# A decoder's first self attention rewritten from pairs of heads to quads of heads, with the rotation's partner shuffled instead of projected

## The chip, the core and the metric

One Trainium2 chip, one of its cores. The metric is device time in microseconds from the first to the last instruction of the launch, as the median of several runs. TensorE runs at one of two granted clocks, 1.2 or 2.4 GHz; the profile gives the mean over a stretch as a share of 2.4 GHz.

## The reference

The kernel computes six blocks of a decoder of depth two on x of shape (8, 256, 256) in float32: each normalises x and adds its result to it. The change touches the first block alone, self attention of 64 query heads of 16 values (4 branches of 16 heads) over 16 key heads that the branches share:

```python
q, k = _rope(q), _rope(k)
scores = einsum('bhtd,bhsd->bhts', q, k) * ATTNSCALE
key_self = clip(sum(k * k, axis=-1), 1e-06, None)
w = softplus(scores / sqrt(key_self)[:, :, None, :])
w = where(causal, w, 0.0)
w = w * sigmoid(SCALE * w)
w = where(w < sinks, 0.0, w)
total = sum(w, axis=-1) + sinks + 1e-06
out = einsum('bhts,bhsd->bhtd', w / total, v) + sinks / total * v_null
y = mean over branches of (out @ W_O + W_O_bias)
```

## The kernel before

`attention0` (lines 247 to 690) first normalises all of x and turns it (`normalise`, which also issues the stage's loads and waits for them in `loaded`), then works through 8 batches with all engines side by side. Every engine has its own in-order list of work; semaphores tie the lists together. A batch's 16 key heads are taken in 8 steps of a **pair of heads**, and two steps make a **quad**.

For each pair there are three score slots (`score_slot`), each two PSUM banks of 512 columns in banks 0 to 5. A slot is two matmuls of 32 rows (L335 or L342: the two heads lie in two row groups of 32 rows, which TensorE can use at the same time) and two matmuls of all 128 rows that add the causal mask (L338, 256 columns, or L345, 512 columns). Each float32 matmul is two instructions in the trace. ScalarE takes each slot with a softplus into the weights `w` (`soften`, L464), and after six slots it loads another table and runs four silu instructions over the quad (L502), then loads the softplus table again. VectorE cuts the weights at the sinks, sixteen instructions for a quad (`threshold`, L674). TensorE then sums over the keys (`sum_half`, L365, four column groups of 32 at once), two halves for a quad.

Beside this main line there are **side items**, which pass through banks 6 and 7: the projections q and k of a batch, projected twice, once as they are and once with the halves of each head swapped (weights `wq` and `wqs`, `wk` and `wks`, L393), which VectorE turns into two products with cosine and sine (L623) and GpSimd adds (L551); v (L400, L631); the norms of the keys (L406, L636, then Ln and Exp on ScalarE, L510 and L512, and L582 on GpSimd); the sums copied by ScalarE (L483), transposed back by TensorE ("regroup", L413) and copied by VectorE (L644, with the totals at L654 and L658); the contexts divided by GpSimd (L570, L577), transposed ("turn", L420, taken by ScalarE at L473) and projected out (L427, L663). Which item goes to TensorE at which step stands in the tables `SENT` and `SENT_LATE`; where VectorE takes it, in `TAKEN`. A bank of side items may be written again when its reader is done (`free`). The batches overlap: a step can hold an item of the batch before (`OLD`) or after (`AHEAD`). The weights `w` have room for four pairs (`PAIR_RING`).

Of the kernel before, what the change touches and what calls it, by code (L numbers as in the profile page):

```python
# [11 lines left out]
ALU = mybir.AluOpType  # L12
# [121 lines left out]
def normalise(nc, norm, x_all, xnT_all, ident, psum, loads, loaded):  # L134

    with ExitStack() as stack:
# [64 lines left out]
PAIRS_OF_HEADS, QUADS, SLOTS = NH // 2, NH // 4, 3  # L201
PAIR_RING = 4
# [16 lines left out]
SENT_LATE = {0: ("regroup", 4, OLD, 6), 1: ("regroup", 5, OLD, 7), 2: ("regroup", 7, OLD, 6), 3: ("norm", 0, AHEAD, 7),  # L219
             4: ("q", 0, AHEAD, 7), 5: ("q", 1, AHEAD, 6), 6: ("q", 3, AHEAD, 7), 7: ("regroup", 2, HERE, 6)}  # L220

SUM_BANKS = {1: (7, 6), 3: (7, 6), 5: (6, 7), 7: (6, 7)}

EVEN_POINTS, ODD_POINTS = 6, 3
TAKEN = {(0, 0): ("regroup", 2, OLD, 6), (0, 1): ("regroup", 3, OLD, 7), (0, 2): ("q", 0, HERE, 6), (0, 3): ("q", 1, HERE, 7),
         (0, 4): ("q", 2, HERE, 6), (0, 5): ("q", 3, HERE, 7), (1, 0): ("regroup", 4, OLD, 6),
         (2, 0): ("regroup", 5, OLD, 7), (2, 1): ("k", 0, AHEAD, 6), (2, 2): ("k", 1, AHEAD, 7), (2, 3): ("v", 0, HERE, 6),
         (2, 4): ("regroup", 6, OLD, 7), (3, 0): ("regroup", 7, OLD, 6),
         (4, 0): ("norm", 0, AHEAD, 7), (4, 4): ("regroup", 0, HERE, 6), (5, 0): ("q", 0, AHEAD, 7),
         (6, 0): ("q", 1, AHEAD, 6), (6, 3): ("out", 0, OLD, 6), (6, 4): ("regroup", 1, HERE, 7), (6, 5): ("q", 2, AHEAD, 6),  # L230
         (7, 0): ("q", 3, AHEAD, 7)}
REGROUPS = 8
ROTATED = 2 + 2 * BR


def rotations(b, kind, i, when):

    place = i if when == HERE else 4 + i if kind == "k" else 6 + i
    return b * ROTATED + 6 + place


def quad_at(b, at, new, old):

    if at >= 0:
        return (at, b * QUADS + at) if new else None
# [2194 lines left out]
```

## Time and profile before

| what | us |
|---|---|
| median of 3 runs | 3093.82 (3092.99 to 3099.23) |
| the profiled execution: its time | 3088.96 |
| its span, first to last instruction | 3087.2 |
| the first attention: last load landed to its last instruction | 29.45 to 925.48 |

The profile's shares of busy time over the whole span are TensorE 88%, VectorE 57%, ScalarE 51%, GpSimd 26%; they average over six blocks with different limits. To read it for this change, take the stretch from 25 to 960 us alone, see which engine is busy in it and what the others wait for, and then follow one quad in the timeline.

### The profile page before, as it was taken

The page shows a single profiled execution, that of the slowest core. Times are in us where ns is not written, and L with a number is a line of the kernel's source. Part 1 is how long each engine was busy: PE and PEld are TensorE (multiplying, and loading weights), DVE is VectorE, ACT ScalarE, POOL GpSimd, SP SyncE. Part 2 cuts the span into 40 slices and gives each one's busy share as a digit, 9 for nine tenths or more (in the row PEclk, how much of TensorE's full clock was granted, in tenths as well). Part 3 has the DMA queues.
Part 4 walks back from the last instruction along what each step waited for, and adds up shares of the span by engine and source line. Part 5 has one row for each costly group of instructions (what it writes and reads, how often), then busy time and mean ns, then how long its engine had stood idle before and what let it go on. Part 6 is the DMA issues. An engine that isn't in the chain of part 4 may idle for free. (4 is left out here: it accounts for less than half of the span.)

```text
span 3087.2 us, 46929 instructions
## 1 busy us (share of the span) xinstructions
PE 2711.5 (88%) x17384; PEld 2026.2 (66%) x17384; DVE 1762.0 (57%) x4040; ACT 1559.8 (51%) x3054; POOL 788.5 (26%) x887
## 2 busy tenths in 40 slices
PE   6889888988867689999979999999979999949998
PEld 3444444544436467776758888888867777748887
DVE  3555545544547566556546666666666565555454
ACT  2665656565645344444435555555555556542221
POOL 1122222212210144444531111111005566610000
PEclk8888988987979799999989999999989999979999
DMA  3000000000002211111010000000010000020000
GB/s 104 4 4 4 1 4 4 4 1 4 1 1 66 77 25 25 30 44 25 22 34 13 6 6 6 3 1 1 1 67 8 6 7 5 1 96 6 6 8 31
DMA packets 88753, 58.80 MB, mean 19 GB/s; under 512 B 55120, under 2 KB 78544, under 8 KB 88016
## 3 DMA queue, kind: packets, MB, share of 16 engines
q1 hardware_dynamic: 88528, 55.80, 6.1%
q8 instruction: 142, 2.33, 0.3%
q14 instruction: 83, 0.68, 0.1%
HBM read 39.00 MB, written 8.39 MB: 15 GB/s over the span
## 5 line engine op out<-in xcount | busy, mean ns | idle before, releaser
L674 DVE SCALAR_TENSOR_TENSOR a_w<-a_w,a_sinks 128x384 f32<-128x384 f32 x512 | 324.2, 698 | 69.8 <-ACT a_w L502 69.8
L464 ACT ACTIVATE a_w<-psum 128x1024 f32<-128x1024 f32 x192 | 190.7, 1026 | 299.4 <-PE psum L338 119.1
L1103 POOL TENSOR_SCALAR f_weights<-f_weights,f_sums 128x256 f32<-128x256 f32 x256 | 232.8, 927 | 271.3 <-DVE f_sums L1333 271.3
L2011 POOL TENSOR_SCALAR x_weights<-x_weights,x_sums 128x256 f32<-128x256 f32 x256 | 232.5, 927 | 271.4 <-DVE x_sums L2070 271.4
L1261 ACT ACTIVATE f_weights<-psum,f_negmax 128x256 f32<-128x256 f32 x256 | 118.0, 473 | 210.3 <-DVE f_negmax L1327 210.3
L1597 ACT ACTIVATE a_turned_w_hi<-psum 128x512 fp32r<-128x512 f32 x256 | 139.1, 595 | 151.7 <-PE psum L1507 151.7
L1981 ACT ACTIVATE x_weights<-x_masked_s,x_negmax 128x256 f32<-128x256 f32 x256 | 127.0, 497 | 136.2 <-DVE x_negmax L2062 136.2
L1713 DVE TENSOR_REDUCE a_negmax<-psum 128x1 f32<-128x1024 f32 x128 | 156.7, 1224 | 64.6 <-PE psum L119 60.5
L502 ACT ACTIVATE a_w<-a_w 128x1536 f32<-128x1536 f32 x128 | 179.4, 1472 | 0.4
L335 PE MATMUL psum<-a_qT,a_kT_half 32*128 32x512 f32 x512 | 160.3, 705 | 15.9 <-ACT a_w L464 13.9
L1675 POOL TENSOR_TENSOR a_xT_lo<-all_xnT_all,a_xT_hi 128x512 fp32r<-128x512 f32 x56 | 71.5, 1277 | 384.8 <-ACT a_xT_hi L1577 384.8
L1720 DVE TENSOR_TENSOR a_turned_w_lo<-psum,a_turned_w_hi 128x512 fp32r<-128x512 f32 x256 | 163.7, 681 | 0.2 <-ACT a_turned_w_hi L1597 0.2
L117 PE MATMUL psum<-a_turned_w_hi,a_v_hi 128*128 128x256 f32 x512 | 150.1, 293 | 0.5 <-DVE a_turned_w_lo L1720 0.5
L118 PE MATMUL psum<-a_turned_w_lo,a_v_hi 128*128 128x256 f32 x512 | 144.8, 283 | 0.0
L119 PE MATMUL psum<-a_turned_w_hi,a_v_lo 128*128 128x256 f32 x512 | 144.8, 283 | 0.0
L1606 ACT ACTIVATE a_weights<-psum,a_negmax 128x1024 f32<-128x1024 f32 x128 | 143.5, 1121 | 2.3 <-DVE a_negmax L1713 2.2
L365 PE MATMUL psum<-a_w,a_v 128*32 128x512 f32 (+1 forms) x1024 | 120.3, 599 | 17.1 <-DVE a_w L674 14.2
L1507 PE MATMUL psum<-all_ident,a_weights 128*128 128x128 f32 x1024 | 132.6, 272 | 0.5 <-ACT a_weights L1606 0.5
L623 DVE SCALAR_TENSOR_TENSOR a_rot<-psum,a_bq,a_rope 128x256 f32<-128x256 f32 x128 | 55.6, 475 | 133.1 <-PE psum L393 133.1
L1507 PEld LDWEIGHTS psum<-all_ident,a_weights 128*128 128x128 f32 x1024 | 119.1, 140 | 17.8 <-ACT a_weights L1606 2.2
L570 POOL TENSOR_TENSOR a_ctxn<-a_ctx,a_vnull 128x256 f32<-128x256 f32 x64 | 45.8, 737 | 296.4 <-DVE a_ctx L644 296.4
L117 PE MATMUL psum<-a_kT_hi,a_qT_hi 128*128 128x512 f32 x256 | 106.5, 416 | 7.9 <-issue 6.9
(359 smaller groups left out, 7464.1 us busy)
## 6 DMA issues: line engine op xcount, KB each, us to landing
f_xnT<-all_xnT_all SPq DMA_DIRECT2D x16, 256.0 KB, 2.4
f_pv_rows<-f_pv SPq DMA_DIRECT2D x8, 512.0 KB, 3.2
f_pv_groups<-f_pv_rows SPq DMA_DIRECT2D x8, 512.0 KB
f_w<-in_f_w SPq DMA_DIRECT2D x2, 2048.0 KB, 9.9
all_x_all<-in_x SPq DMA_DIRECT2D x1, 2048.0 KB, 8.6
a_xnT<-all_xnT_all SPq DMA_DIRECT2D x8, 256.0 KB, 2.3
x_xnT<-all_xnT_all SPq DMA_DIRECT2D x8, 256.0 KB, 2.3
x_ctxT<-in_x_ctxT SPq DMA_DIRECT2D x8, 256.0 KB, 2.9
```

The source lines that it names most:

```text
L117: pe.matmul(out, lhsT[0], rhs[0], start=start, stop=False)
L118: pe.matmul(out, lhsT[0], rhs[1], start=False, stop=False)
L119: return pe.matmul(out, lhsT[1], rhs[0], start=False, stop=stop)
L335: pe.matmul(psum[:, 2 * x + h, :], kT_half[rows[h], step % 2, g, 0:P], qT[rows[h], g, 2 * x:2 * x + 2, :], start=True, stop=False)
L464: act.activation(to, of, ACT.Softplus).then_inc(softened, 1)
L502: act.activation(wu, wu, ACT.Silu, scale=SILU_SCALE).then_inc(silu_done, 1)
L674: ins = dve.scalar_tensor_tensor(part, part, sinks[:, col:col + 1], part, ALU.is_ge, ALU.mult)
L1103: ins = pool.tensor_scalar(w, w, sums[:, k, h, t:t + 1], None, ALU.mult)
L1507: ins = pe.transpose(psum[:, 4 + half, j * P:(j + 1) * P], weights[u % 2][:, lo:lo + P], ident[:])
L1713: dve.tensor_reduce(negmax[:, u % STAT_RING:u % STAT_RING + 1], psum[:, 2 * (u % 2):2 * (u % 2) + 2, :].rearrange("p a n -> p (a n)"), AX. ...
L1720: dve.tensor_tensor(lo, psum[:, 4 + half, :].rearrange("p (j t) -> p j t", t=P), hi.bitcast(F32), ALU.subtract)\
L2011: ins = pool.tensor_scalar(w, w, sums[:, k, h, t:t + 1], None, ALU.mult)
```

## The change

The first attention is issued anew; what it computes stays. One iteration m is now a whole quad of heads (`ALL_QUADS` = 32).

- **Score groups.** Three groups of four banks each (`scores`): four matmuls of 32 rows in the four row groups, into four banks, then four mask matmuls. `heads_of` pairs heads so that a quad's heads lie in the four row groups. Groups 0 and 2 of quad m use four banks (`banks_of(m)`), group 1 and the next quad's group 0 the other four. All eight banks serve scores; the number of instructions for scores stays.
- **Side items** now use fixed banks inside the four that the quad's last group has left (`beside_quad`, "first" before the sums and "last" after them), and every group of scores claims all four of its banks: it waits until softplus or the side items' readers have left them (`claim`).
- **The ring** of weights is 3 quads (4 pairs before). The sums of quad m - 1 are made in iteration m.
- **Rotation.** The swapped projections, their weights and their loads are gone. VectorE swaps the halves of each head out of PSUM with one shuffle instruction of 128x512 for two chunks (`stream_shuffle`), then makes the products; the bank is free after the first two of four products (`proj_taken`). GpSimd adds two chunks in one instruction.
- ScalarE takes the sums after silu, and names the silu table load; v is projected from `xnT_all` itself, and SyncE's copy into `xnT` is gone; the output projection is two items of one tile.

The diff, cut to its core:

```diff
-PAIRS_OF_HEADS, QUADS, SLOTS = NH // 2, NH // 4, 3
-PAIR_RING = 4
+QUADS, SLOTS = NH // 4, 6
+QUAD_RING = 3
...
-SENT = {0: [("regroup", 3, OLD, 7), ("q", 0, HERE, 6), ("q", 1, HERE, 7), ("q", 2, HERE, 6), ("q", 3, HERE, 7)],
-        2: [("k", 0, AHEAD, 6), ("k", 1, AHEAD, 7), ("v", 0, HERE, 6), ("regroup", 6, OLD, 7)],
-        4: [("turn", 0, OLD, 6), ("turn", 1, OLD, 7), ("turn", 2, OLD, 6), ("turn", 3, OLD, 7), ("regroup", 0, HERE, 6)],
-        6: [("out", 0, OLD, 6), ("regroup", 1, HERE, 7), ("q", 2, AHEAD, 6)]}
...
-SUM_BANKS = {1: (7, 6), 3: (7, 6), 5: (6, 7), 7: (6, 7)}
...
+ALL_QUADS = B * QUADS
...
+SWAP = [u // DH * DH + (u + DH // 2) % DH for u in range(32)]
...
+def heads_of(k):
+
+    return slice(8 * (k // 2) + k % 2, 8 * (k // 2) + 8, 2)
...
+def banks_of(m):
+
+    return m % 2 * 4
...
+def beside_quad(m):
+
...
+    if k == 0:
+        sent = [[("regroup", m - 2, 0, 0), ("regroup", m - 2, 1, 1), ("q", b, 2, 2)], [("out", b - 2, 1, 1)]]
+    elif k == 1:
+        sent = [[("v", b, 0, 0), ("q", b, 3, 1), ("regroup", m - 2, 0, 2)], [("regroup", m - 2, 1, 1), ("k", b + 1, 0, 2)]]
+    elif k == 2:
+        sent = [[("turn", b - 1, 0, 0), ("turn", b - 1, 1, 1), ("norm", b + 1, 0, 2)],
+                [("turn", b - 1, 2, 1), ("turn", b - 1, 3, 2), ("regroup", m - 2, 0, 3), ("regroup", m - 2, 1, 0),
+                 ("q", b + 1, 0, 1)]]
+    else:
+        sent = [[("regroup", m - 2, 0, 0), ("regroup", m - 2, 1, 1), ("q", b + 1, 1, 2)], [("out", b - 1, 0, 1)]]
+    made = lambda kind, of: 0 <= of < (ALL_QUADS if kind == "regroup" else B)
+    return [[(kind, of, i, banks_of(m) + bank) for kind, of, i, bank in part if made(kind, of)] for part in sent]
+
+
+SUM_BANKS = 3, 0
+SPAN = range(1 - QUADS, ALL_QUADS + QUADS + 1)
+
+TURNED_AT = {item[:3]: n for n, item in enumerate(
+    item for m in SPAN for part in beside_quad(m) for item in part if item[0] in "qk")}
 
 
 def attention0(nc, norm, x_all, xnT_all, ident, psum, a):
     with ExitStack() as stack:
         s = Scope(nc, stack, "a0")
-        wq, wqs = s.sb("wq", [P, CC, BR * D]), s.sb("wqs", [P, CC, BR * D])
-        wk, wks, wv = s.sb("wk", [P, CC, D]), s.sb("wks", [P, CC, D]), s.sb("wv", [P, CC, D])
...
-        @block.sync
-        def _(sp):
-            for b in range(B):
-
-                sp.wait_ge(v_done, b)
-                sp.dma_start(xnT[:], xnT_all[:, bass.ds(b, 1), :, :]).then_inc(v_x_here, 16)
-
...
+            free = {}
+
+            def claim(banks, taken):
+
+                last = {}
...
+            def scores(m, group):
+
+
+                b, k = divmod(m, QUADS)
+                g, base = k // 2, banks_of(m + group % 2)
+                if group == 0 and k % 2 == 0:
+                    pe.wait_ge(kheads_ready, b * 2 + g + 1)
+                if group < 2 and k % 2 == 0:
+                    pe.wait_ge(rotated, TURNED_AT["q", b, 2 * g + group] + 1)
+                claim(range(base, base + 4), lambda bank: (softened, m * SLOTS + 2 * group + (bank - base) // 2 + 1))
+                rows = [slice(32 * j, 32 * j + 32) for j in range(4)]
+                for j in range(4):
+                    keys, at = (slice(0, P), qT[rows[j], g, 2 * group:2 * group + 2, :]) if group < 2 else \
+                        (slice(P, T), qT[rows[j], g, :, P:T])
+                    pe.matmul(psum[:, base + j, :], kT_half[rows[j], k % 2, g, keys], at, start=True, stop=False)
+                for j in range(4):
+                    by_branch = psum[:, base + j, :].rearrange("p (r t) -> p r t", r=2 if group < 2 else BR)[:, :, 0:P]
+                    ins = pe.matmul(by_branch, ident_r[:], future[:].unsqueeze(1).to_broadcast([P, by_branch.shape[1], P]),
+                                    start=False, stop=True)
                 ins.then_inc(scored, 1)
...
+            def sum_half(n, half):
+                b, k = divmod(n, QUADS)
...
+                bank = banks_of(n + 1) + SUM_BANKS[half]
+                claim([bank], lambda _: (sums_taken, 2 * n + half + 1))
...
+            def send(kind, of, i, bank):
+                spare = psum[:, bank, :]
+                if kind in "qk":
+                    n = TURNED_AT[kind, of, i]
+                    claim([bank], lambda _: (proj_taken, n + 1))
+                    for z in range(2):
+                        weights, lo = (wk, z * P) if kind == "k" else (wq, (2 * (2 * (i % 2) + z) + i // 2) * P)
+                        for c in range(CC):
+                            ins = pe.matmul(spare[:, z * T:(z + 1) * T], weights[:, c, lo:lo + P], xnT_all[:, of, c, :],
+                                            start=(c == 0), stop=(c == CC - 1))
+                    ins.then_inc(projected, 1)
...
+                elif kind == "turn":
+                    if i == 0:
+                        pe.wait_ge(ctx_ready, of * QUADS + QUADS)
+                    claim([bank], lambda _: (turn_taken, of * 4 + i + 1))
+                    for q in range(4):
+                        lo = 8 * (4 * (i % 2) + q)
+                        ins = pe.transpose(spare[:, q * P:(q + 1) * P],
+                                           ctxn[:, i // 2, lo:lo + 8, :].rearrange("p h d -> p (h d)"), ident[:])
+                    ins.then_inc(turn_done, 1)
+                else:
+                    pe.wait_ge(turn_taken, of * 4 + 2 * i + 2)
+                    claim([bank], lambda _: (out_taken, 2 * of + i + 1))
+                    for q in range(8):
+                        ins = pe.matmul(spare[:, 0:D], ctxT[:, i, q, :], wo[:, q, :], start=(q == 0), stop=(q == 7))
+                    ins.then_inc(out_done, 1)
...
+            for m in SPAN:
+                here, before = 0 <= m < ALL_QUADS, 0 <= m - 1 < ALL_QUADS
+                first, last = beside_quad(m)
+                if here:
+                    scores(m, 1)
+                    scores(m, 2)
+                if 0 <= m < ALL_QUADS - 1:
+                    scores(m + 1, 0)
+                for item in first:
+                    send(*item)
+                if before:
+                    for half in range(2):
+                        sum_half(m - 1, half)
+                for item in last:
+                    send(*item)
+                if m == -1:
+                    scores(0, 0)
...
+                group, pair = x // 2, x % 2
+                if x == 0:
+                    wait(act, summed, 2 * (m - QUAD_RING) + 2)
+                if pair == 0:
+                    act.wait_ge(scored, m * GROUPS_OF_SCORES + group + 1)
+                wu = w[:, m % QUAD_RING, 2 * pair:2 * pair + 2]
+                bank = banks_of(m + group % 2) + 2 * pair
+                of = psum[:, bank:bank + 2, :]
...
+            for m in SPAN:
+                here, before = 0 <= m < ALL_QUADS, 0 <= m - 1 < ALL_QUADS
+                turns = [item for part in beside_quad(m) for item in part if item[0] == "turn"]
+                if here:
                     for x in range(SLOTS):
-                        if new:
...
-
-            over_batches(act, body)
+                        soften(m, x)
+                if here:
+                    act.preload_act_table_set("silu_and_others")
+                    act.wait_ge(softened, m * SLOTS + SLOTS)
+                for j in range(4):
+                    if here:
+                        wj = w[:, m % QUAD_RING, j].rearrange("p r t -> p (r t)")
+                        act.activation(wj, wj, ACT.Silu, scale=SILU_SCALE).then_inc(silu_done, 1)
+                    if j == 0:
+                        for _, b, i, bank in turns[:2]:
+                            take_turned(b, i, bank)
+                    if before and j == (1 if m % QUADS == 2 else 3):
+                        for half in range(2):
+                            take_sums(m - 1, half)
+                    if j == 1:
+                        for _, b, i, bank in turns[2:]:
+                            take_turned(b, i, bank)
+                ahead = m // QUADS + 1
+                if m % QUADS == 2 and ahead < B:
+                    act.preload_act_table_set("natural_log_exp_and_others")
+                    act.wait_ge(norm_taken, ahead + 1)
+                    act.activation(ksq[:], ksq[:], ACT.Ln).then_inc(ln_k, 1)
+                    act.wait_ge(ln_k, ahead + 1)
+                    act.activation(ksq[:], ksq[:], ACT.Exp, scale=-0.5, bias=ln_quarter[:, 0:1]).then_inc(knorm_ready, 1)
+                if here or m % QUADS == 2 and ahead < B:
+                    act.preload_act_table_set("softplus")
...
+            for m in SPAN:
+                b, k = divmod(m, QUADS)
+                sent = beside_quad(m)
+                if k == 0 and b < B:
+                    head_rows(b, 1)
+                if k == 3 and b + 1 < B:
+                    alone(pool, knorm_ready, b + 2, passed)
+                    pool.tensor_tensor(kT[:], kT[:], ksq[:], ALU.mult).then_inc(knormed, 1)
+                    head_rows(b + 1, 0)
...
+                    n = TURNED_AT[kind, of, i]
+                    bias, cols = (bk, (0, 1)) if kind == "k" else (bq, [2 * (2 * (i % 2) + z) + i // 2 for z in range(2)])
+                    dve.wait_ge(projected, n + 1)
+                    dve.stream_shuffle(swap[:, n % 2, :], spare, SWAP).then_inc(swapped, 1)
+
+                    wait(dve, rotated, n - 1)
+                    for z in range(2):
+                        part = slice(z * T, (z + 1) * T)
+                        ins = dve.scalar_tensor_tensor(rot[n % 2][:, 0, part], spare[:, part], bias[:, 0, cols[z]:cols[z] + 1],
+                                                       rope[:, 0, :], ALU.add, ALU.mult)
+                    ins.then_inc(proj_taken, 1)
+                    dve.wait_ge(swapped, n + 1)
+                    for z in range(2):
+                        part = slice(z * T, (z + 1) * T)
+                        ins = dve.scalar_tensor_tensor(rot[n % 2][:, 1, part], swap[:, n % 2, part], bias[:, 1, cols[z]:cols[z] + 1],
+                                                       rope[:, 1, :], ALU.add, ALU.mult)
                     ins.then_inc(rot_made, 1)
...
+            for m in SPAN:
+                here = 0 <= m < ALL_QUADS
+                first, last = ([item for item in part if item[0] != "turn"] for part in beside_quad(m))
+                for item in first:
+                    take(*item)
+                for j in range(2):
+                    if here:
+                        threshold(m, j)
+                for item in last:
+                    take(*item)
+                for j in range(2, 4):
+                    if here:
+                        threshold(m, j)
```

## Rows read from the trace of the kernel before

**Rows 1.** Stretches: whole stage, steady part, next stage; busy us, TensorE clock (PEclk)
```profile
core 0: us, PE busy (x) PEld busy (x) DVE busy (x) ACT busy (x) POOL busy (x), PEclk, DMA share, GB/s
25.00:960.00 935.00, 779.13 (x3627) 414.90 (x3628) 472.08 (x942) 540.84 (x547) 197.91 (x272) 0.85 0.02 7
380.00:490.00 110.00, 96.55 (x456) 50.04 (x448) 55.87 (x108) 65.94 (x64) 25.04 (x34) 0.84 0.01 3
930.00:1130.00 200.00, 148.69 (x748) 114.57 (x750) 127.09 (x297) 89.82 (x295) 42.77 (x38) 0.85 0.20 59
```

**Rows 2.** L582 from 300 us: ns min/median/max, first and last start
```profile
L582 POOL TENSOR_TENSOR a_kT<-a_kT,a_ksq x5: 1262/1262/1263, 314.5 to 748.0; 128x512 f32<-128x512 f32 x5
```

**Rows 3.** Groups by line, 380 to 820 us: busy us, mean ns, idle before
```profile
L674 DVE SCALAR_TENSOR_TENSOR a_w<-a_w,a_sinks 128x384 f32<-128x384 f32 x256 | 163.0, 701 | 19.7 <-ACT a_w L502 19.7
L464 ACT ACTIVATE a_w<-psum 128x1024 f32<-128x1024 f32 x97 | 96.4, 1026 | 161.4 <-PE psum L338 56.6 <-PE psum L345 55.2 <-PE psum L365 49.3
L502 ACT ACTIVATE a_w<-a_w 128x1536 f32<-128x1536 f32 x65 | 91.2, 1472 | 0.2
L335 PE MATMUL psum<-a_qT,a_kT_half 32*128 32x512 f32 x260 | 80.9, 701 | 0.0
...
L623 DVE SCALAR_TENSOR_TENSOR a_rot<-psum,a_bq,a_rope 128x256 f32<-128x256 f32 x64 | 27.9, 476 | 66.4 <-PE psum L393 66.4
...
L644 DVE COPY a_ctx<-psum 128x272 f32<-128x272 f32 x33 | 14.3, 434 | 78.3 <-PE psum L413 78.3
...
L636 DVE TENSOR_SCALAR a_ksq<-psum 128x512 f32<-128x512 f32 x4 | 2.8, 692 | 45.3 <-PE psum L406 45.3
```

**Rows 4.** The timeline of ScalarE: start, length; a table load, silu, softplus
```profile
574.86 1.28 ACT L502 ACT_TABLE_LOAD   x1
576.16 5.61 ACT L502 ACTIVATE a_w<-a_w 128x1536 f32<-128x1536 f32 x4
...
583.07 2.85 ACT L464 ACTIVATE a_w<-psum 128x1024 f32<-128x1024 f32 x3
```

**Rows 5.** The timeline of TensorE where the granted clock is 2.4 GHz
```profile
563.91 1.13 PE L335 MATMUL psum<-a_qT,a_kT_half 32*128 32x512 f32 x4
564.97 0.50 PE L338 MATMUL psum<-a_future,a_ident_r 128*128 128x256 f32 x2
565.31 1.02 PE L393 MATMUL psum<-all_xnT_all,a_wq 128*128 128x256 f32 x4
566.17 1.03 PE L393 MATMUL psum<-all_xnT_all,a_wqs 128*128 128x256 f32 x4
567.13 1.13 PE L342 MATMUL psum<-a_qT,a_kT_half 32*128 32x512 f32 x4
568.19 0.73 PE L345 MATMUL psum<-a_future,a_ident_r 128*128 128x512 f32 x2
568.85 1.50 PE L365 MATMUL psum<-a_w,a_v 128*32 128x512 f32 x16
```

**Rows 6.** The timeline of TensorE where the granted clock is 1.2 GHz
```profile
504.79 1.12 PE L413 MATMUL psum<-all_ident,a_sumT 128*128 128x128 f32 x4 [1.46 <-DVE a_v L631]
...
511.71 2.08 PE L335 MATMUL psum<-a_qT,a_kT_half 32*128 32x512 f32 x4
513.72 0.80 PE L338 MATMUL psum<-a_future,a_ident_r 128*128 128x256 f32 x2
514.45 2.76 PE L365 MATMUL psum<-a_w,a_v 128*32 128x512 f32 x16
```

**Rows 7.** The timeline at the stage's start and at its end
```profile
29.45 2.07 PE L393 MATMUL psum<-all_xnT_all,a_wk 128*128 128x256 f32 x4 [4.98 <-DMA a_bo<-in_a_bo]
...
51.29 1.13 PE L335 MATMUL psum<-a_qT,a_kT_half 32*128 32x512 f32 x4 [1.97 <-POOL a_qT L551]
...
893.24 7.74 DVE L674 SCALAR_TENSOR_TENSOR a_w<-a_w,a_sinks 128x384 f32<-128x384 f32 x12
...
924.79 0.69 DVE L663 SCALAR_TENSOR_TENSOR all_x_all<-psum,all_x_all 128x512 f32<-128x512 f32 x1 [15.07 <-PE psum L427]
```

More of the change, by code:

```diff
@@ L232 @@
[L232 to L245, printed above, removed]
-    return (QUADS + at, b * QUADS + at) if old else None
+ALL_QUADS = B * QUADS
+SWAP = [u // DH * DH + (u + DH // 2) % DH for u in range(32)]
+FIRST, LAST = range(2)
+GROUPS_OF_SCORES = 3
+def heads_of(k):
+    return slice(8 * (k // 2) + k % 2, 8 * (k // 2) + 8, 2)
@@ L266, in attention0 @@
         ln_quarter = s.sb("ln_quarter", [P, 1])
[L267 to L268 removed]
+        swap = s.sb("swap", [P, 2, 2 * T])
+        rot = [s.sb(f"rot{i}", [P, 2, 2 * T]) for i in range(2)]
         qT = s.sb("qT", [P, CC, BR, T])
@@ new lines, in _ @@
+            free = {}
+            def claim(banks, taken):
+                last = {}
+                for bank in banks:
+                    if bank in free:
+                        sem, value = free[bank]
+                        last[sem.name] = (sem, max(value, last.get(sem.name, (sem, 0))[1]))
+                for sem, value in last.values():
+                    pe.wait_ge(sem, value)
+                for bank in banks:
+                    free[bank] = taken(bank)
+            def scores(m, group):
[15 more added lines that the diff above has]
+                                    start=False, stop=True)
@@ L347, in score_slot @@
                 ins.then_inc(scored, 1)
-            free = {}
-            def sum_half(b, quad, half, bank):
-                k, n = quad
+            def sum_half(n, half):
+                b, k = divmod(n, QUADS)
                 if k == 0 and half == 0:
@@ L356, in sum_half @@
                 pe.wait_ge(weights_done, n + 1)
[L357 to L359 removed]
+                bank = banks_of(n + 1) + SUM_BANKS[half]
+                claim([bank], lambda _: (sums_taken, 2 * n + half + 1))
+                heads = range(NH)[heads_of(k)]
                 for tile in range(TT):
[L361 to L363 removed]
+                    for j in range(4):
+                        branches = w[:, n % QUAD_RING, j, 2 * half:2 * half + 2, :]
+                        out = psum[VCOLS * j:VCOLS * j + VCOLS, bank, :].rearrange("p (r t) -> p r t", r=2)
@@ new lines, in _ @@
+            for m in SPAN:
+                b, k = divmod(m, QUADS)
+                sent = beside_quad(m)
[5 more added lines that the diff above has]
+                    head_rows(b + 1, 0)
+                if k == 1 and 0 <= b - 1 < B:
+                    x_b = x_all[:, (b - 1) * TT:b * TT, :]
+                    pool.tensor_tensor(x_b, x_b, bo[:, 0:1, :].to_broadcast([P, TT, D]), ALU.add).then_inc(x_biased, 1)
+                for part in sent:
+                    for kind, of, i, _ in part:
+                        if kind in "qk":
+                            rotate(kind, of, i)
+                        elif (kind, i) == ("regroup", 1):
+                            finish_context(of)
```

383 lines of the change are left out of this document (104 added, 279 removed).

## The prediction

> **What bounds the kernel now.** I read the page first (which engine is busy, and how much of the span the first attention takes), then the stage cut into stretches, then the groups by line, then the timeline of one batch. In the steady part of the stage TensorE is busy 96.6 of 110 us, ScalarE 65.9, VectorE 55.9, and TensorE's mean clock is 0.84 [rows 1]: it changes between the two levels, 2.4 and 1.2 GHz, and stands at the lower one for 32% of the time. What the other engines wait for is TensorE: the softplus waits 161 us of 440 for it, and most of VectorE's idle time ends with a projection or a transpose [rows 3]. So TensorE's work, stretched by its clock, bounds the stage. The period of a batch is (748.0 - 314.5) / 4 = 108.4 us [rows 2].
>
> **TensorE's work, part by part** (at 2.4 GHz first, spacing of starts in the timeline). A slot of two heads takes 1.06 us for its four instructions of 32 rows and 0.34 for two masks of 256 columns, 0.66 for two of 512 [rows 5]. The two heads already overlap: 260 instructions of 701 ns make only 80.9 us of busy time [rows 3]. A batch has 16 slots of 1.40 and 8 of 1.72: 36.2 us. The change puts four heads into the four row groups. No row shows four row groups at once. The bounds: 1.06 (they overlap as two do) and 2.12 (two by two); I take 1.1, because the four column groups of the sums do overlap fourfold: sixteen instructions in 1.50 us, where one instruction of 256 full columns takes 0.215 and these stream 384 on average in each of four groups [rows 5]. Groups 0 and 1 then cost 1.1 + 0.68 = 1.8 and group 2 1.1 + 1.3 = 2.4; a batch 8 x 1.8 + 4 x 2.4 = 24, 12 less.
> The swapped projections go: ten chunks of 0.86 [rows 5], 8.6 us a batch. The plain ones stay, 1.72 for a q or k item. The rest stays: sums 2 x 1.45 a quad, v 1.72, norm 0.86, a regroup or a turn about 0.5 each, out 2 x 3.45 (32 instructions of 0.215), these by columns from the 0.215. In all TensorE goes from about 81 to 60 us a batch at 2.4 GHz. At 1.2 GHz the same rows are 2.0 for a slot's scores, 0.75 for two masks, 2.76 for a half of the sums [rows 6]: about twice.
>
> **ScalarE's work** stays: 24 softplus of 1.03 (three in a row take 2.85), 16 silu of 1.40, nine table loads of 1.28, the copies [rows 3, 4]; 65 us a batch. The Trainium skill, TensorEngine Tiling (Array Packing), section Performance Considerations, warns that tiling "speeds up TensorE but not PSUM evacuation". The row agrees as far as it goes, the same 24 softplus instructions being left; by that rule alone a batch could not fall below ScalarE's 65 us, and it does not in my sum.
>
> **VectorE's work.** Thresholds: 163.0 / 256 = 0.637 us each, 2.55 a head, 40.8 a batch [rows 3]. The products stay 20 of 0.44 to 0.48. Added: five shuffles of 128x512 out of PSUM. No row shows one; nearest are the 128x512 out of PSUM at 0.69 (I take that) and, as the lower end, the copy of 272 elements at 0.43 [rows 3]; the upper end is twice the 0.69. That is 3.5 us a batch (2.2 to 6.9). VectorE comes to about 59 us a batch. The skill, VectorE: DVE Perf Modes, section The perf-mode tier table (the rule you actually need), gives about 2400 ns for a shuffle of 2048 elements; an estimate from it is 0.6 us for 512, and the sum would be 4 us shorter over eight batches. GpSimd adds the same bytes in fewer instructions; it is busy 25 of 110 [rows 1] and hides that.
>
> **What is late next.** No engine is full by its work (TensorE 60, ScalarE 65, VectorE 59), so the new waits decide. All eight banks now serve scores, and group 1 of quad m + 1 needs the four banks that the side items of quad m use: it waits until VectorE has taken the last of them, and VectorE takes that only after two heads' thresholds of quad m. This makes one loop for a quad. From S, when those banks are free, at 2.4 GHz: groups 1 and 2 until S + 4.2; the next quad's group 0 until 6.0; group 2's softplus until 6.1; first items on TensorE from 6.1; silu of the first head done at 8.9 (table load 1.28 [rows 4]). On VectorE until S + 5.1 the old quad's last two thresholds (hidden behind the scores). Then, by quad of the batch:
> First (k = 0) two regroups (0.43, and about 1.1 with the totals, an estimate from that copy and as much again and a half) and q: TensorE done at 9.1, shuffle and four products until 11.5, two thresholds until 16.6, an output item 0.5: 17.2.
> Second (k = 1): v, q, a regroup until 12.6, two thresholds until 17.7, the second regroup 1.1, then k, whose bank is free after the shuffle and two products, 1.6: 20.4.
> Third (k = 2): VectorE would be done at 17.1, but ScalarE has its turns (4 x 0.54), Ln, Exp and one more table here: it begins the next quad at 20.4, and the fourth quad's group 1 is softened 3.4 later than its scores allow: 20.5.
> Fourth (k = 3), as the first: 17.2.
> A batch takes 75.3 us at 2.4 GHz. With TensorE at 1.2 GHz throughout, scores and items are late and the sums push the last items: first items start at S + 11.1, and the same count gives 29, 30, 29 and 29, **117 us**.
> The clock lies between. At the share of the lower clock of now, 32%, the period is 75.3 + 0.32 x 41.7 = **88.6 us**. TensorE would be busy 60 x 1.32 / 88.6 = 89% of it, as it is now (88%), and the next stage has a clock of 0.85 with TensorE busy 74% [rows 1]. That is why I take 0.84 again. Against it: once a quad TensorE has sent its last items by about S + 15.3 and stands still for 2 to 5 us, where now all its idle time is 13 us of 110 [rows 1].
>
> **The sum.** Start: loads end at 29.45 and hold TensorE for 5.0 us; 1.25 of some 5 MB (by their shapes) less on the queue can save up to 4.5. Then only k and one q item instead of k and four q chunks twice stand before the first scores. They start at 51.3 [rows 7]; I take 42 (38 to 49). End: from the last thresholds (893.2) to 925.5 is 32 us [rows 7]; this tail is a chain and stays. Between lie 893.2 - 51.3 = 842 us, 7.77 periods of 108.4. So the stage ends at 42 + 7.77 x 88.6 + 32 = 762 instead of 925.5: 163 less. The profiled execution's 3089.0 becomes 2926; the median of the runs is 4.9 above it: **2930**. Nothing behind the stage changes; its rows are untouched. SyncE's copy that goes waits for nobody's path: 0.
>
> **The rivals.**
> (a) The clock. It gives most of the spread. Never low: 7.77 x 75.3, 103 us less, 2827. Low for 60% of the time: period 100.3, 3021.
> (b) The four row groups go two by two, so that the edit doesn't do what it says. Each group costs 1.06 more at 2.4 GHz; three groups stand before the first items, which adds 2.9 a quad there and twice that at the lower clock: period 86.9 to 140, at 32% 104; 3050. For it: nothing shows four; against it: the fourfold sums.
> (c) Slower than before. The loop through the banks leaves TensorE standing once a quad, its clock falls in each of these gaps and stays down for the scores and items that come next. From a share of 0.83 of the time at 1.2 GHz on (period 109.8) the stage is longer than now; at the full share it is 7.77 x 117 + 74 = 983, 57 more: 3151. For it: after a gap of 1.46 us at 504.8 the scores, masks and sums take the long form until 517 us [rows 6]. Against it: in (c) TensorE would be busy without a gap, and busy stretches are where the clock is high now.
>
> **How the numbers follow.** Forecast, 2870 to 2990 (low clock 15 to 50% of the time): 0.62, at 2930. Clock nearly always high, about 2827 to 2870: 0.09. Low 50 to 80%, 2990 to 3080: 0.13. (b), 3020 to 3080: 0.10. (c): 0.06. The range leaves out (c), the upper part of (b) and the lowest edge: **2835 to 3050**. A measurement can tell about 0.2% (6 us) from no change. Faster by more: 0.93; within: 0.01; slower: 0.06.
>
> **What would show it.** In the changed kernel's timeline four instructions of 32 rows should start within some tens of ns, and a group's eight take about 1.2 us at 2.4 GHz (right) or 2.2 (rival b). No swapped projection; a shuffle near 0.69 us. The period by L582's successor: 85 to 92. ScalarE should wait for group 1's scores (the loop), little for group 0's. In the stretches the clock should be 0.75 to 0.92 and TensorE's busy share 80 to 90%. The prediction is wrong if softplus waits for group 0, if VectorE's thresholds wait for ScalarE rather than follow the side items, or if the tail exceeds 35 us.

## The result and the profile after

The changed kernel takes 2866.3 us (2861.1 to 2867.2) where the kernel before takes 3093.4 in the same runs: a ratio of 0.9258 with a 95% interval of 0.9242 to 0.9274, 227 us less. The forecast was 2930, in a range of 2835 to 3050. The profiled execution has a span of 2859.1 us. The next block's first load is issued at 704.70 instead of 925.76, so 221 of the 228 us between the two spans were saved in the first attention. The other 7 lie in the third block, whose code is untouched: from its first load (1032.66 before, 811.42 after) to that of the fourth (1586.19, 1357.76) it takes 553.5 us before and 546.3 after, and 544 to 549 in the profiles of the experiments. What moves it is not known, so differences below of under some 10 us say little.

First the changed kernel's stretches (busy us and count per engine, the TensorE clock, DMA share, GB/s), which answer to [rows 1]: the whole stage, then its steady part. Behind them the line of GpSimd that occurs once a batch, as in [rows 2].

```profile
core 0: us, PE busy (x) PEld busy (x) DVE busy (x) ACT busy (x) POOL busy (x), PEclk, DMA share, GB/s
25.00:710.00 685.00, 526.62 (x3232) 304.35 (x3232) 513.48 (x980) 518.49 (x507) 198.49 (x224) 0.89 0.01 2
200.00:640.00 440.00, 350.96 (x2217) 203.22 (x2212) 346.53 (x653) 351.41 (x343) 132.27 (x148) 0.91 0.00 1
```

```profile
L561 POOL TENSOR_TENSOR a_kT<-a_kT,a_ksq x5: 1572/1572/1575, 259.1 to 581.6; 128x512 f32<-128x512 f32 x5
```

The period is (581.6 - 259.1) / 4 = 80.6 us instead of 108.4. The forecast had 85 to 92. TensorE, ScalarE and VectorE are now busy alike, 80%, 80% and 79% of the steady part, and TensorE's clock is 0.91 where it was 0.84. A clock of 0.91 means that it stands at 1.2 GHz for 2 x (1 - 0.91) = 18% of the time; before it was 32%.

The groups by line in the steady part (busy us, mean ns, idle before and its releasers), which answer to [rows 3]:

```profile
L654 DVE SCALAR_TENSOR_TENSOR a_w<-a_w,a_sinks 128x384 f32<-128x384 f32 x353 | 238.1, 740 | 3.7 <-ACT a_w L484 3.0
L455 ACT ACTIVATE a_w<-psum 128x1024 f32<-128x1024 f32 x132 | 127.5, 1023 | 87.1 <-PE psum L349 86.8
...
L346 PE MATMUL psum<-a_qT,a_kT_half 32*128 32x512 f32 x533 | 97.0, 799 | 89.0 <-issue 25.5 <-DVE a_rot L603 25.3 <-ACT a_w L455 18.7
...
L598 DVE STREAM_SHUFFLE a_swap<-psum 128x512 f32<-128x512 f32 x27 | 20.0, 741 | 0.0
```

The thresholds now hardly wait for silu (3.7 us of 440); the scores (L346) wait 89 us for banks; the softplus's one releaser is the mask matmul of its own group. The shuffle takes 741 ns. The timeline of ScalarE tells which group it is. In order, the softplus of group 0, group 1 and group 2 of one quad:

```profile
394.33 1.94 ACT L455 ACTIVATE a_w<-psum 128x1024 f32<-128x1024 f32 x2
402.15 1.94 ACT L455 ACTIVATE a_w<-psum 128x1024 f32<-128x1024 f32 x2 [5.88 <-PE psum L349]
404.35 1.94 ACT L455 ACTIVATE a_w<-psum 128x1024 f32<-128x1024 f32 x2 [0.25 <-PE psum L349]
```

Group 0 does not wait, group 1 waits 5.88 us. In this batch it waits in three quads of four (2.35, 5.88 and 3.02 us); in the one between, ScalarE itself is late. This is the loop that was forecast, and the timeline of TensorE shows one turn of it (start, length, idle before and releaser), from group 1 of one quad to group 1 of the next:

```profile
379.15 1.14 PE L346 MATMUL psum<-a_qT,a_kT_half 32*128 32x512 f32 x8 [2.90 <-issue]
...
383.09 1.14 PE L346 MATMUL psum<-a_qT,a_kT_half 32*128 32x512 f32 x8
...
391.93 1.89 PE L378 MATMUL psum<-all_xnT_all,a_wk 128*128 128x256 f32 x8
398.87 2.09 PE L346 MATMUL psum<-a_qT,a_kT_half 32*128 32x512 f32 x8 [5.05 <-DVE a_rot L603]
400.89 1.22 PE L349 MATMUL psum<-a_future,a_ident_r 128*128 128x256 f32 x4
402.04 1.14 PE L346 MATMUL psum<-a_qT,a_kT_half 32*128 32x512 f32 x8
```

Eight instructions in four row groups take 1.14 us, as long as four in two row groups (1.13 [rows 5]). TensorE sends the last item (k, 391.93), stands still 5.05 us until VectorE has emptied its bank (`proj_taken`, L603), and the scores behind the gap run at half speed (2.09), those 3 us later at full speed (1.14). I had not forecast this quick rise, and the experiments turn on it.

### The profile page after: what moved, and what is told of

Read it like the earlier page. It is cut to its first block and busy times, and to the rows that moved or that the text cites. A ratio compares the mean times of both kernels' runs of the same rounds, so it can differ in the third digit from the quotient of the medians.

```text
span 2859.1 us, 46204 instructions
## 1 busy us (share of the span) xinstructions
PE 2470.4 (86%) x17064; PEld 1925.7 (67%) x17064; DVE 1819.9 (64%) x4128; ACT 1550.4 (54%) x3054; POOL 787.6 (28%) x839
## 5 line engine op out<-in xcount | busy, mean ns | idle before, releaser
L654 DVE SCALAR_TENSOR_TENSOR a_w<-a_w,a_sinks 128x384 f32<-128x384 f32 x512 | 343.7, 738 | 10.9 <-ACT a_w L484 9.9
L346 PE MATMUL psum<-a_qT,a_kT_half 32*128 32x512 f32 x768 | 140.3, 807 | 129.6 <-DVE a_rot L603 36.5
L346 PEld LDWEIGHTS psum<-a_qT,a_kT_half 32*128 32x128 f32 x768 | 37.4, 224 | 162.1 <-issue 114.6
L349 PEld LDWEIGHTS psum<-a_future,a_ident_r 128*128 128x128 f32 x384 | 69.1, 231 | 101.2 <-issue 97.1
```

Of the source, the lines that this page charges most:

```text
L346: pe.matmul(psum[:, base + j, :], kT_half[rows[j], k % 2, g, keys], at, start=True, stop=False)
L654: ins = dve.scalar_tensor_tensor(part, part, sinks[:, col:col + 1], part, ALU.is_ge, ALU.mult)
```

## The experiments

Each time below is the median, compared through the ratio to the kernel before measured in the same runs; 0.001 of ratio is 3.1 us.

**Undo one part of the change.** The loop theory sums waits; so first the parts were taken away one at a time. In the kernel before, only the shuffle instead of the swapped projections:

```diff
-                        for v, weights in enumerate((wk, wks) if kind == "k" else (wq, wqs)):
+                        for v, weights in enumerate((wk,) if kind == "k" else (wq,)):
...
+                    dve.stream_shuffle(swap[:, i % 2, :], ps[:, 0, :], SWAP).then_inc(swapped, 1)
```

> One part of the change alone, in the kernel before: the swapped projections are gone (their weights are still loaded) and VectorE swaps the halves of each head out of PSUM, ten shuffles of 128x256 a batch; pairs, banks and order stay. Theory (before the change TensorE's work, stretched by its clock, bounds the stage): 8.6 us a batch less at 2.4 GHz, times 1.31 for the low clock's share, 11 us a batch, 60 to 90 us less in all, and the rest of the 227 us belongs to the quads. Rival (the side items were hidden, the gain is all from the quads): 0 to 30 us less. A second rival (VectorE's added 4.5 us a batch and its longer takes hold the two side banks): slower by up to 30 us.

It took 3108.6 us, ratio 1.0056 (1.0041 to 1.0071): 17 us slower than before, with 8.6 us a batch less work for TensorE. So the statement that TensorE's work bounds the kernel before was wrong as it stood. Its first attention alone ended 28.7 us later (954.47 instead of 925.76), the blocks behind it took 11 less, 9 of them in the third. The clock went down with the work. The kernel before, then this one:

```profile
380.00:820.00 440.00, 385.46 (x1799) 200.56 (x1791) 224.97 (x436) 264.13 (x256) 99.19 (x137) 0.84 0.01 3
380.00:820.00 440.00, 364.01 (x1605) 170.99 (x1606) 229.95 (x499) 254.13 (x247) 97.11 (x132) 0.80 0.01 3
```

0.80 is 40% of the time at 1.2 GHz, 0.84 is 32%. In the changed kernel the opposite, every projection sent twice:

```diff
-                    for z in range(2):
+                    for z in (0, 1, 0, 1):
```

> The changed kernel, with every q and k item's eight instructions sent twice over into the same bank: TensorE's work comes back (8.6 us a batch at 2.4 GHz), VectorE's and the banks' stay as changed. Loop theory (a quad is bound by the loop scores, softplus, side items, VectorE's takes and thresholds, banks free): the item's longer time counts where VectorE waits for it, 1.7 us in three quads and about 1 in the third, 6 us a batch, 47 us in all. Rival (TensorE's work still bounds): 8.6 x 1.18 = 10 us a batch, 79 us and more. If neither counts: under 15 us.

2884.9 us, ratio 0.9333 (0.9318 to 0.9348): 0.0075 or 23 us more than changed, half of the 47 that the loop theory expected. TensorE's clock was 0.93 instead of 0.91. TensorE's work does not bound the changed kernel either, and adding some of it lifted the clock.

**Two row groups instead of four**, the same instructions in another order:

```diff
-                for j in range(4):
-                    keys, at = ...
-                for j in range(4):
-                    by_branch = ...
+                for pair in ((0, 1), (2, 3)):
+                    for j in pair:
+                        keys, at = ...
+                    for j in pair:
+                        by_branch = ...
```

> The changed kernel, with each group's matmuls sent as before in pairs: two of 32 rows, their two masks, then the other two. The overlap over four row groups is taken away, nothing else. Theory: each group costs 1.06 us more at 2.4 GHz, three groups stand before the first side items of the next quad, 3.2 us a quad, 12.7 a batch, 99 us in all (110 to 120 with the clock). Rival (ScalarE or VectorE bounds and the scores are hidden): under 30 us.

3166.2 us, ratio 1.024 (1.0216 to 1.0264): 0.098 or 304 us more than the changed kernel, some three times the 99 to 120 expected, and slower than the kernel before. Its timeline of TensorE shows why:

```profile
390.26 1.79 PE L347 MATMUL psum<-a_qT,a_kT_half 32*128 32x512 f32 x4 [2.24 <-DVE all_x_all L647]
391.98 0.80 PE L350 MATMUL psum<-a_future,a_ident_r 128*128 128x256 f32 x2
392.71 2.08 PE L347 MATMUL psum<-a_qT,a_kT_half 32*128 32x512 f32 x4
...
404.50 2.08 PE L347 MATMUL psum<-a_qT,a_kT_half 32*128 32x512 f32 x4
406.50 0.80 PE L350 MATMUL psum<-a_future,a_ident_r 128*128 128x256 f32 x2
```

TensorE works from 390.26 to 407 without a gap, and from the second on every pair takes the half-speed 2.08 us. With four row groups the clock rose 3 us after such a gap; with two it did not rise in 17. The mean clock was 0.68, a low share of 0.64:

```profile
380.00:820.00 440.00, 389.00 (x1471) 190.99 (x1469) 228.33 (x438) 232.29 (x223) 89.86 (x102) 0.68 0.00 1
```

Here the forecast's own formula holds: with 12.7 us a batch more, 88 us at 2.4 GHz and 142 at 1.2, a share of 0.64 gives 123 us; measured was (849.6 - 242.0) / 5 = 121.5. At the changed kernel's share of 0.18 it would be 98. By this formula, so as an estimate, some 17 of the 41 us a batch are the lost overlap and some 24 the clock.

**The loop through VectorE.** The last side items taken after four heads' thresholds, and after one, instead of after two:

```diff
-                for j in range(2):
+                for j in range(4):      # late; early: range(1)
                     if here:
                         threshold(m, j)
                 for item in last:
                     take(*item)
-                for j in range(2, 4):
+                for j in range(4, 4):   # late; early: range(1, 4)
```

> The changed kernel, with VectorE taking the last side items after the thresholds of all four heads instead of after two. No work is added, only the time at which the banks come free. Loop theory: the banks of a quad come free 8 x 0.67 = 5.4 us later in three quads of a batch and some 2 in the one where ScalarE is late, 18 us a batch, about 140 us in all, and ScalarE's wait for group 1's scores grows by that. Rival (TensorE's or ScalarE's work bounds, the order of VectorE's list does not matter): within 15 us of the changed kernel.

> The changed kernel, with VectorE taking the last side items after the thresholds of one head instead of two. Loop theory: the banks come free 2.7 us earlier in the second quad of a batch and about 1.5 in the first and fourth (there the output item is ready only shortly before), not at all earlier in what ScalarE holds up in the third; 5 us a batch, some 40 us less than the changed kernel. Rival (what the late version cost came from the thresholds standing before the sums, not from the banks): within 10 us of the changed kernel, or slower, since three heads' thresholds then stand before the next quad's first items.

Late: 2984.2 us, ratio 0.9656 (0.964 to 0.9673), 123 us more than changed. Early: 2807.2 us, ratio 0.9069 (0.9049 to 0.909), 58 us less. No work was added or taken away. ScalarE's waits from 200 to 640 us (total, times, longest) are, in the changed kernel, the late and the early version:

```profile
ACT a_w L455 <- PE psum L349: 86.8, 39, 5.9
```

```profile
ACT a_w L455 <- PE psum L349: 146.5, 35, 10.1
```

```profile
ACT a_w L455 <- PE psum L349: 38.9, 41, 3.5
```

The late version's banks come free later and ScalarE's wait for the scores grows; the early version's shrinks. The rival, that VectorE's order doesn't matter, falls. But not all of it is the loop's own length: the longer gaps of the late version also lowered TensorE's clock, to 0.83 from 0.91, and the early version raised it to 0.95. The late version:

```profile
200.00:640.00 440.00, 303.47 (x1804) 171.80 (x1802) 266.94 (x532) 285.60 (x278) 107.00 (x126) 0.83 0.00 1
```

A low share of 0.34 instead of 0.18 makes 6.7 us a batch by the forecast's 41.7 us between its two periods, an estimate; the period grew by 18.4 (99.0 instead of 80.6). For the early version it is 3.3 of 8.9. The expectations had left the clock out. The early version beats both kernels; ScalarE is busy 89% of its steady part and the period is 71.7 us:

```profile
200.00:520.00 320.00, 275.05 (x1810) 162.13 (x1812) 283.26 (x535) 286.03 (x280) 110.73 (x125) 0.95 0.00 1
L561 POOL TENSOR_TENSOR a_kT<-a_kT,a_ksq x5: 1572/1578/1581, 249.7 to 536.6; 128x512 f32<-128x512 f32 x5
```

**The clock in the gaps.** Unread matmuls over all rows at the end of the loop:

```diff
+                if here and m % QUADS != 2 and m > 0:
+                    pe.wait_ge(sums_taken, 2 * m)
+                    for again in range(4 if m % QUADS == 1 else 2):
+                        for c in range(CC):
+                            pe.matmul(psum[:, banks_of(m), 0:T], wq[:, c, 0:P], xnT_all[:, 0, c, :],
+                                      start=(c == 0), stop=(c == CC - 1))
```

> The changed kernel, with matmuls that nobody reads sent in the gap at the end of the loop, while TensorE waits for the banks: 3.4 us at 2.4 GHz in the second quad, 1.7 in the first and fourth, none in the third, over all 128 rows. Theory (the clock falls in these gaps and the next scores pay for it): the low clock's share goes from 0.20 to under 0.10 and 4 us a batch come back, 20 to 40 us less. Rival (the low stretches lie where they cost nothing, or the filler is late): 0 to 20 us more.

2839.2 us, ratio 0.9172 (0.915 to 0.9194): 27 us less by adding work, as expected. The clock from 200 to 520 us was 0.96. The same filler in the one gap left in the early version (two repeats, second quad only):

> The version with the last side items taken after one head, with 1.7 us of unread matmuls in the one gap of 2.9 us that is left, at the end of the second quad of a batch. Clock theory: that quad's next scores run at 2.4 GHz instead of 1.2 and some 1 to 2 us a batch come back, 8 to 15 us less than 2807. Rival (ScalarE, busy 89% of the time, is the bound now): within 5 us of 2807.

2813.4 us, ratio 0.9096 (0.9077 to 0.9115): no gain over 0.9069, and the clock over 200 to 520 us was 0.94 instead of 0.95. A miss for the clock theory: here the filler did not lift the clock. That ScalarE's bound left nothing to be had fits, but is not shown.

**What lifts the clock.** Two ladders of unread float32 matmuls of 512 columns, back to back, ahead of the stage's work. They serve for their traces, not for their time.

```diff
+            for groups, times in (("all", 12), (2, 16), (4, 16), (1, 16), (4, 16), (2, 16), ("all", 12)):
+                for _ in range(times):
+                    for j in range(1 if groups == "all" else groups):
+                        part = slice(0, P) if groups == "all" else slice(32 * j, 32 * j + 32)
+                        pe.matmul(psum[:, j, :], xnT_all[part, 0, 0, 0:P], xnT_all[part, 1, :, :], start=True, stop=True)
```

> The changed kernel, with a ladder of float32 matmuls of 512 columns ahead of the first attention's work, back to back, read by nobody: all rows, then two row groups of 32, four, one, four, two, all rows again. Theory (after two runs more: while only two row groups work TensorE's clock falls to or stays at 1.2 GHz though it never stands still, and with four groups or all rows it rises): the clock is 2.4 in the first stretch once it has risen, 1.2 in both stretches of two groups and in the one of one group, and 2.4 in those of four groups and of all rows. Rival (only standing still lets it fall): 2.4 GHz throughout after the first few us.

Stretches of it: in the first run of two row groups, in the run of one (and the start of the four behind it), in the run of four that follows:

```profile
41.00:53.00 12.00, 12.00 (x60) 5.35 (x58) 0.00 (x0) 0.00 (x0) 0.00 (x0) 1.00 0.00 1
71.50:91.00 19.50, 19.50 (x28) 7.39 (x27) 0.00 (x0) 0.00 (x0) 0.00 (x0) 0.50 0.00 0
95.00:106.00 11.00, 11.00 (x108) 6.28 (x104) 0.00 (x0) 0.00 (x0) 0.00 (x0) 1.00 0.01 1
```

TensorE is busy in all of each. One row group brought the clock down to 0.50 and four brought it back, but two held 1.00, against my expectation. The rival, that only standing still lets the clock fall, fails by the run of one. Both stretches of two had begun high. The second ladder begins each stretch low, after twelve matmuls in one row group (`one(12)`; `fours` are the four row groups, `left` and `right` the operands):

```diff
+            one(12)
+            for _ in range(32):
+                for j in range(2):
+                    pe.matmul(psum[:, j, :], left(fours[j]), right(fours[j]), start=True, stop=True)
+            one(12)     # then the same with masks, then four, then four with masks
```

> A second ladder, since in the first two row groups side by side held the clock at 2.4 GHz when they found it there, against what I had expected. Now each stretch starts low, after twelve matmuls in one row group (which brought the clock down in the first ladder): two row groups, two row groups with two masks after each pair (as the scores were), four row groups, four with four masks. Theory (two groups hold the clock they find but do not lift it; four lift it): 1.2 GHz to the end of both stretches of two, 2.4 after a few us in both of four. Rival (two lift it as four do, and something else kept the clock low in the kernels that send pairs): 2.4 after a few us in all four stretches.

In order: two; two with masks; four, from its first us on; four with masks, its first 8 us and the rest:

```profile
57.00:112.00 55.00, 55.00 (x128) 26.47 (x126) 0.00 (x0) 0.00 (x0) 0.00 (x0) 0.50 0.00 0
132.00:176.00 44.00, 44.00 (x97) 15.95 (x94) 0.00 (x0) 0.00 (x0) 0.00 (x0) 0.50 0.00 0
196.50:200.00 3.50, 3.50 (x25) 1.86 (x24) 0.00 (x0) 0.00 (x0) 0.00 (x0) 0.66 0.00 0
200.00:211.00 11.00, 11.00 (x105) 6.27 (x98) 0.00 (x0) 0.00 (x0) 0.00 (x0) 1.00 0.01 1
226.00:234.00 8.00, 8.00 (x31) 3.59 (x33) 0.00 (x0) 0.00 (x0) 0.00 (x0) 0.56 0.00 0
234.00:247.00 13.00, 13.00 (x94) 6.20 (x87) 0.00 (x0) 0.00 (x0) 0.00 (x0) 1.00 0.01 1
```

Two row groups work for 55 us, and with masks for 44 us, without a gap at 1.2 GHz; four come up in both their stretches. The theory with its correction (two hold what they find, four lift) holds in all four; the rival, that two lift the clock as four do, fails in both stretches of two. The ladders vary how many row groups work at once, and with it how many instructions TensorE finishes in a microsecond; which of the two counts for the clock they can't tell.

**The same in the kernels.** Four instructions over all rows, unread, ahead of each group of the kernel with pairs:

```diff
+                for c in range(CC):
+                    pe.matmul(psum[:, base, 0:T], wq[:, c, 0:P], xnT_all[:, 0, c, :], start=(c == 0), stop=(c == CC - 1))
```

> The kernel with the groups sent two row groups at a time (300 us slower than the changed kernel), and with four instructions over all 128 rows, read by nobody, ahead of each group of scores: 0.86 us at 2.4 GHz each, 10 us a batch more for TensorE. Theory (the long stretches of two row groups hold the clock at 1.2 GHz): the full-row work lifts the low clock's share from 0.67 to under 0.5, which pays for it, so that the time is within 40 us of the 3166 in spite of 10 us a batch more work, or below it. Rival (the clock does not depend on the rows in use): 3166 plus 7.8 x 10 x 1.67, about 130 us more.

3127.6 us, ratio 1.011 (1.008 to 1.0139), against 1.024 without them: 40 us less with 10 us a batch more work; the clock over 380 to 820 us went from 0.68 to 0.82. And the kernel before with the shuffle, given its TensorE work back:

```diff
-                        for v, weights in enumerate((wk,) if kind == "k" else (wq,)):
+                        for again, weights in enumerate((wk, wk) if kind == "k" else (wq, wq)):
                             for c in range(CC):
-                                ins = pe.matmul(spare[:, v * T:(v + 1) * T],
+                                ins = pe.matmul(spare[:, 0:T],
```

> The kernel before with VectorE's shuffle, which was 17 us slower than before, and now each plain projection sent twice over into the same half bank: TensorE's work is that of the kernel before again, VectorE's longer takes stay. Clock theory (taking the projections away left TensorE standing more and its clock lower, share 0.40 instead of 0.28): the low share goes back to about 0.3, and the time is at or below the 3109 with 8.6 us a batch more work. Rival (VectorE's longer takes of the two side banks made it slower, and TensorE's work counts): 3109 plus 8.6 x 1.4 x 7.8, about 90 us more.

3084.8 us, ratio 0.9971 (0.9958 to 0.9983): 26 us less than without the repeated projections, where the rival expected 90 more.

```profile
380.00:820.00 440.00, 384.56 (x1868) 204.00 (x1868) 246.04 (x531) 270.59 (x261) 104.03 (x143) 0.89 0.01 3
```

The clock is 0.89 instead of 0.80, a low share of 0.22 where 0.3 was expected. VectorE's longer takes alone are thus not what made the shuffle slower, since this kernel has them too. They do have a part in it. TensorE's waits from 380 to 820 us for a projection's bank that VectorE still reads (total, times, longest), in the kernel before, with the shuffle, and with the projections repeated:

```profile
PE psum L393 <- DVE a_rot L623: 11.4, 4, 2.9
PE psum L395 <- DVE a_rot L628: 22.8, 8, 4.1
PE psum L395 <- DVE a_rot L628: 13.5, 8, 3.3
```

The periods of a batch, by the starts of the GpSimd line that occurs once in each, are 108.4, 111.8 and 105.8 us, of which TensorE is busy 95.0, 92.5 and 92.5 and stands still 13.4, 19.3 and 13.3. So between the last two kernels the lower clock stretched the smaller work to the same busy time, and the 6.0 us of difference are TensorE's idle time. With less to send, TensorE runs into VectorE's takes, stands still longer and has the lower clock; work put back fills the gap. In what way the clock began to fall (which gap, or which pair of scores that did not lift it again) was not taken apart further.

## Why the prediction was right, and where its working was not

- **Sign, range and mechanism**: right. The loop scores, softplus, side items, VectorE, banks binds the changed kernel, and the late and early versions moved it by 123 and 58 us where 140 and 40 were expected, part of both through the clock. ScalarE waits for group 1 and not for group 0, and the thresholds do not wait for it, as the signs asked.
- **"What bounds the kernel now"**: wrong as it stood. TensorE's busy time was the largest, but taking 10% of its work away made the kernel 17 us slower and sending it twice made it 26 us faster again. Of the 8.6 us a batch taken out, only 2.5 left TensorE's busy time (95.0 to 92.5), because the clock fell; its idle time grew by 5.9. So a high busy share did not mean that less work would be less time. What bounds the kernel before in its place, beyond this, stays open.
- **Four row groups**, taken at 1.1 us: 1.14 with its tail, 1.07 by the spacing of starts. Rival (b) did not come. The kernel that sends two by two, the nearest to it, took 3166 where (b) had 3050. The Trainium skill, TensorEngine Tiling (Array Packing), section Theoretical Speedup, gives up to fourfold for 32 rows, and the trace agrees: at 1.2 GHz in the second ladder 23 instructions in one row group took 19.83 us, 0.86 each, and eight in four row groups 2.09, 0.26 each, 3.3 times as fast.
- **Each quad's turn at 2.4 GHz** (17.2, 20.4, 20.5, 17.2, in all 75.3): group 1 of successive quads starts at 379.15, 398.87, 416.57, 439.13, 458.28, so 19.7, 17.7, 22.6, 19.2. The projection of k at 391.93 marks the first of these as the batch's second quad; against the forecast it is second 19.7 for 20.4, third 17.7 for 20.5, fourth 22.6 for 17.2, first 19.2 for 17.2. That ScalarE is late shows, but one quad after the one to which the forecast gave it; the two together are 40.3 where 37.7 stood. The sum is 79.1 in this batch, stretches at 1.2 GHz included, so that 75.3 was not measured by itself. One term was too short: a threshold takes 238.1 / 353 = 0.674 us, not 0.637, 2.4 us a batch more.
- **The low clock's share, 32%**: this is the term that was mis-sized. It was 18%. The formula at 0.18 gives 75.3 + 0.18 x 41.7 = 82.8 us, and 80.6 was measured where 88.6 was forecast. The stage was forecast to end at 762.4 and ended at 704.4, 58 us earlier: 60 less between the first scores and the last thresholds (628.0 instead of 688.4), 4 more at the start, 2 less in the tail. The 7 us behind the stage, put at nothing, make it 65 of the profiled execution. That the formula with 0.18 lands 2.2 us a batch too long while it leaves out the longer thresholds shows that its 75.3 and 117 are not exact either. I argued the share from TensorE's busy share (89%; it was 80%), which would rather have spoken for a lower clock. What decided was how many row groups the scores use at once: with four the clock was up again 3 to 6 us after each gap in which it had fallen (398.87 to 402.04, 439.13 to 444.62), with two it stayed low for 17 us and more. The Trainium skill, TensorE: Matmul & The Clock Gate, section Terms, has the clock set by how busy TensorE is; the ladders show TensorE busy without a gap at either clock, so busy time in the profile is not enough to tell it.
- **Rival (c)**, slower through gaps and clock, needs a low share of 0.83. Not reached (0.18); but with pairs the share was 0.64 and the kernel slower than before, and by the formula it would not have been at a share of 0.18 (98 us a batch against 108.4), so the mechanism that (c) names is real.
- **The start**: loads landed at 25.69 instead of 29.45, 3.8 us less (up to 4.5 forecast); the first scores began at 46.4 instead of 51.3 (42 forecast). **The tail**, from the last thresholds: 674.39 to 704.43, 30.0 us (32 forecast). It is counted here from the last eight thresholds, in the forecast from the last twelve, so the two are only roughly alike.
- **The shuffle**: 0.741 us, 0.69 taken. The estimate of 0.6 us, from the figure for 2048 elements in the Trainium skill, VectorE: DVE Perf Modes, section The perf-mode tier table (the rule you actually need), was further off; the measurement decides.

```profile
25.69 1.99 PE L378 MATMUL psum<-all_xnT_all,a_wk 128*128 128x256 f32 x8 [1.19 <-DMA a_bo<-in_a_bo]
...
46.40 1.50 PE L346 MATMUL psum<-a_qT,a_kT_half 32*128 32x512 f32 x8 [4.52 <-POOL a_kT_half L513]
```

## What to carry to other kernels

Before work is taken off TensorE, look at its clock in the profile: where short gaps meet matmuls of few rows, the work that looks superfluous can be what fills the gaps and holds the clock up, and the saving is paid back. Send narrow matmuls so that all four row groups work together; here the order alone was worth 304 us, some three fifths of it, by the estimate above, through the clock. And where engines share banks in a loop, move the reader that frees them ahead of work that nobody waits for: two lines on VectorE were worth 58 us.

## What was not expected of the hardware

In the ladders TensorE's clock went by how many row groups worked at once and by where it had stood. Back to back and without a gap, float32 matmuls of 512 columns in one row group of 32 rows brought it from 2.4 to 1.2 GHz; in two row groups at once they kept 2.4 GHz for 12 us where they found it and 1.2 GHz for 55 us where they found that; in four row groups they lifted it in every stretch. Unread matmuls made three kernels faster: by 27 us in the gaps of the changed kernel, by 40 ahead of pairs of scores, by 26 in the side items of the kernel before with the shuffle. In the early version they did not help.

Going back and forth between row groups and all rows has a price. At 1.2 GHz, four instructions in two row groups take 1.75 us when sent back to back (127 in 55.50 us); with masks over all rows between them the mask starts 2.01 us after them (135.12 to 137.13, and so throughout). Where these 0.26 us go no run shows.
